# Second attention of a two-layer block: the weighting of the values issued for two key tiles at a time

## The reference, cut to what matters

```python
q = input_tensor @ wq.T + bq          # the same for k and v
q = q.reshape(B, S, H, D).transpose(0, 2, 1, 3)
scores = jnp.einsum('bhsd,bhtd->bhst', q, k) / jnp.sqrt(jnp.float32(D))
attn = jax.nn.softmax(scores, axis=-1)
out = jnp.einsum('bhst,bhtd->bhsd', attn, v)
out = out.transpose(0, 2, 1, 3).reshape(B, S, E)
return out @ wo.T + bo
```

## Time and profile before

| what | value |
|---|---|
| median of 3 runs | 2039.92 us (2038.96 to 2041.53) |
| profiled execution, its own time | 2040.23 us |
| profiled execution, span from first to last instruction | 2038.5 us |
| busy share of the span: PE, PEld, DVE, ACT, POOL | 93%, 72%, 71%, 63%, 32% |
| first weighting of the second attention starts at | 1441.24 us |
| last call of `weigh` inside a group starts at | 2016.66 us |

### The profile page before, as it was taken

The page is one execution under the profiler, slowest core; times in us unless marked ns, Lnnn a source line. Parts: engine busy times, 40 slices in busy tenths (PEclk is TensorE's granted clock), DMA queues, the critical chain, the costliest instruction groups (busy, mean ns, idle before and its releaser), DMA issues. The chain is left out here.

```text
span 2038.5 us, 33530 instructions
## 1 busy us (share of the span) xinstructions
PE 1894.3 (93%) x12080; PEld 1465.6 (72%) x12080; DVE 1445.4 (71%) x2916; ACT 1282.9 (63%) x3061; POOL 648.3 (32%) x1021
## 2 busy tenths in 40 slices
PE   1999999999999999999999789997999999999997
PEld 1888878878888888787788568885555655655653
DVE  5785885886868868858768554445777777777773
ACT  3675674665756756746657465543777677777784
POOL 0353453543543534535435413221001111111112
PEclk9999999999999999999999999996999999999999
DMA  6110211111102111111111293321001011011001
GB/s 228 42 42 22 53 42 32 42 32 43 42 22 52 42 27 47 43 32 42 32 36 41 71 335 132 109 86 52 22 1 52 1 52 52 1 52 52 1 32 42
DMA packets 75204, 111.29 MB, mean 55 GB/s; under 512 B 8224, under 2 KB 49568, under 8 KB 74528
## 3 DMA queue, kind: packets, MB, share of 16 engines
q1 hardware_dynamic: 75040, 109.14, 18.3%
HBM read 54.59 MB, written 20.97 MB: 37 GB/s over the span
## 5 line engine op out<-in xcount | busy, mean ns | idle before, releaser
L1565 DVE TENSOR_REDUCE nm<-ps 128x1 f32<-128x512 f32 x512 | 337.0, 687 | 118.5 <-PE ps L1433 114.2
L1659 ACT ACTIVATE pt<-pst 128x512 f32<-128x512 f32 x512 | 296.8, 602 | 144.5 <-PE pst L1441 143.0
L805 POOL TENSOR_SCALAR pr<-pr,rinv 128x128 f32<-128x128 f32 (+3 forms) x512 | 263.1, 533 | 373.7 <-DVE rinv L693 373.7
L573 ACT ACTIVATE pr<-sc,nmax 128x128 f32<-128x128 f32 (+3 forms) x512 | 268.1, 527 | 142.3 <-DVE nmax L682 140.9
L682 DVE TENSOR_REDUCE nmax<-sc 128x1 f32<-128x128 f32 (+3 forms) x512 | 223.0, 484 | 75.4 <-PE sc L409 75.3
L1433 PE MATMUL ps<-kb,qb 96*128 96x512 f32 x512 | 239.8, 471 | 13.5 <-DVE nm L1565 11.2
L811 POOL TENSOR_TENSOR qk<-ra,rb 128x256 f32<-128x256 f32 x256 | 183.0, 735 | 206.8 <-DVE rb L704 171.7
L1441 PE MATMUL pst<-qb,kb 128*128 128x512 f32 x512 | 208.2, 408 | 6.8 <-ACT pt L1659 3.4
L1433 PEld LDWEIGHTS ps<-kb,qb 96*128 96x128 f32 x512 | 98.7, 193 | 145.3 <-issue 84.0
L421 PE MATMUL w<-ident,pr 128*128 128x128 f32 x1280 | 170.6, 280 | 25.6 <-DVE rb L704 19.7
L383 PE MATMUL w<-wq_hi,xt_hi 128*128 128x384 f32 x512 | 183.6, 359 | 2.8 <-DVE xt_lo L676 1.5
(11 more groups left out here) (212 smaller groups left out, 4552.9 us busy)
## 6 DMA issues: line engine op xcount, KB each, us to landing
k<-k SPq DMA_DIRECT2D x256, 128.0 KB, 2.2
raw<-in_w SPq DMA_DIRECT2D x16, 640.0 KB, 5.9
raw<-in_w SPq DMA_DIRECT2D x8, 704.0 KB, 4.2
xa<-in_x SPq DMA_DIRECT2D x2, 2048.0 KB, 13.7
x<-in_x SPq DMA_DIRECT2D x8, 512.0 KB, 3.9
x_scratch<-x SPq DMA_DIRECT2D x8, 512.0 KB, 2.9
xt_hi_scratch<-xt_hi SPq DMA_DIRECT2D x1, 4096.0 KB, 14.6
xt_lo_scratch<-xt_lo SPq DMA_DIRECT2D x1, 4096.0 KB, 23.8
```

The lines of the kernel that those rows point to most:

```text
L573: act.activation(pr[:, h, SOFF[i]:SOFF[i] + (i + 1) * P], sc[:, bank, at:at + (i + 1) * P], ACT.Exp, bias=nmax[:, h, i:i + 1], accum_out=r ...
L805: pool.tensor_scalar(p, p, rinv[:, h, i:i + 1], 1.0, ALU.mult, ALU.mult).then_inc(scaled, 1)
L1565: dve.tensor_reduce(nm[:, g % 2, i, h:h + 1], ps[:, i % 2, :], AXX, ALU.max, negate=True).then_inc(max_done, 1)
L1659: act.activation(pt[:, g % 2, h, i, :], pst[:, i % 2, :], ACT.Exp).then_inc(exp_done, 1)
```

## The change

`weigh` is called only behind heads 1 and 3 of a group, each time for the two key tiles h-1 and h in a row, where before it was called behind each head for the key tile h. The calls, their operands and waits, and the order of the key tiles stay; no other instruction moves against another, and the four calls behind the last group stay as they are.

```diff
@@ -1528,8 +1528,9 @@
                                     if i < 2 and not last:
                                         pe.wait_ge(stack_done, 6 * (q + 2) + 5 + i)
                                     out_project(b - 1, i)
-                        if back1:
-                            weigh(q - 1, (g + 3) % NG1, h, b + 1 if g else b)
+                        if back1 and h % 2:
+                            for kt in (h - 1, h):
+                                weigh(q - 1, (g + 3) % NG1, kt, b + 1 if g else b)
 
                 for j in range(4):
                     turn_z(0, j, (qn_done, 2 * NT) if j < 2 else (stack_done, j - 1))
```

## The result

The changed kernel took 2043.95 us (median of 20 runs, 2038.14 to 2047.51) against 2040.03 us for the kernel before in the same sessions (20 runs). The ratio is 1.0018, 95% interval 1.0011 to 1.0025: slower by 3.9 us, interval 2.2 to 5.1. The forecast was 2046, slower by 5.9; that lies inside the stated range of 2037 to 2053 and above the measured interval.

What follows compares the result with a forecast made beforehand. No engine alone was taken as the bound: three pass two banks each to and fro, and long weighting bursts starve the other two. Half-group changes sum to +0.76 us a batch, times 7.75 is 5.9 on 2040.0: 2046 us, range 2037 to 2053.

Steps and rivals of the forecast that it cites:

- The double burst, 1.86, and 0.34 us saved a merge: TensorE: two weightings in a row take 1.86 us to the next start, saving 0.14 plus 0.20 of edges.
- rival 1: TensorE alone sets the pace, 0.34 us saved at each of 62 merges: 2019 us; chance 0.13 in whole or part.
- Second half of a plain group 7.80, since the casts lose their cover: Heads 2 and 3, groups 3 and 0: ScalarE's casts delay head 3's exponentials and `pst`, 7.80 against 7.15, +0.65 us.
- The walk: Second half of a plain group followed from the double burst's start through ScalarE's casts and exponentials: next burst at 7.80 us.
- First half of a plain group 8.71 by ScalarE's chain: Heads 0 and 1: the 0.52 wait for VectorE goes, ScalarE's copies and exponentials set 8.71 against 9.23, -0.52 us.
- Group 1's second half 14.46: Half with three projections: casts and head 3's exponential make the third `pst` wait until 12.70; 14.46 against 13.79, +0.67 us.
- Its first half 11.2: Group 1, heads 0 and 1: -0.52 plus some 0.4 for ScalarE's later `vs` copy, -0.1 from 11.31 us.
- Group 3's first half no change: Heads 0 and 1 of group 3: the same ScalarE chain gives 8.71 against 8.69 us, 0.0.
- Group 2's second half +0.05: Half with four output projections: TensorE has enough own work to stand over the casts; +0.05 on 9.90 us.
- Times 7.75 batches: The +0.76 us a batch was multiplied by 7.75 batches (31 groups) to 5.9 us; last group and tail unchanged.
- Rival 2: Gain and loss cancel: the same walk with second halves at +0.45 instead of +0.65, 2041 us; chance 0.18.
- Rival 3: Longer burst covered nowhere: second halves +0.86, first halves no gain, +27, 2067 us; chance 0.09 in whole or part.

Runs made afterwards that it cites:

- light kernels: Kernel before and changed kernel, each with VectorE's maxima and ScalarE's exponentials over only 256 of 512 columns: 2018.8 us with single weightings, 2009.75 us merged.
- run 3: Changed kernel with ScalarE's four casts of head 3 moved from ahead of that head's first exponential to behind its second: 2035.38 us against 2040.62 for the kernel before.
- run 4: Kernel before, single weightings kept, with ScalarE's four casts moved behind the second exponential of head 3: 2047.64 against 2040.62 us, ratio 1.0037.
- light kernel with the casts out of the way: Changed kernel with maxima and exponentials over 256 of 512 columns and ScalarE's casts behind head 3's second exponential: 2001.06 us, ratio 0.981 to the kernel before.
- light single kernel: Kernel before, weighting behind each head, with maxima and exponentials over only 256 of 512 columns: 2018.8 us, ratio 0.989.
- run 1: Kernel before with only heads 0 and 1 merged, tiles 2 and 3 still alone behind heads 2 and 3: 2040.4 against 2040.62 us, ratio 1.0004.
- light merged kernel: Changed kernel with maxima and exponentials over only 256 of 512 columns: 2009.75 us, ratio 0.9851 to the kernel before.

## Why the prediction was right, step by step

- *The double burst, 1.86, and 0.34 us saved a merge.* The 1.86 is right. The 0.34 was too much: the light kernels show 0.21 between heads 2 and 3, 0.32 between heads 0 and 1, and with a wait that goes 0.27 as the mean of a batch. It isn't a term of the forecast's sum; it stands in rival 1 and in the bounds.
- *Second half of a plain group 7.80, since the casts lose their cover.* Right: 7.78, with the wait at the `pst` matmuls of head 3 as said, one `pst` earlier than the step I wrote down as decisive. The walk had the fourth `pst` wait until 7.35 and the burst come 0.45 behind it; in the trace the third waits until 6.86, the fourth starts at 7.44 without a wait of its own, and the burst comes 0.34 behind it. That the total fits to 0.02 is partly luck, since the two errors cancel. Runs 3 and 4 show that the casts are the cause of most of it; the length of the burst has a part too, by way of VectorE (run 3).
- *First half of a plain group 8.71 by ScalarE's chain.* Right: 8.72. The stall for VectorE is gone as said.
- *Group 1's second half 14.46.* Right: 14.44, with the third `pst` of head 3 as the waiting one, at 12.67 for 12.70. *Its first half 11.2*: 11.21, though the 0.4 for the `vs` copy was my estimate, and no run tests it by itself. *Group 3's first half no change*: 8.72 for 8.69.
- *Group 2's second half +0.05.* Mis-sized: 9.83, -0.07. There I had only chosen between bounds. With it the batch is +0.62 in place of +0.76.
- *Times 7.75 batches.* This was the larger error for the traces. The six whole batches give 3.7 us, and the last one with the tail 0.6; in it the last three groups, with less other work, got shorter by 0.8, and the four last calls come 0.86 later behind the last pair. The first one came out shorter, 73.2 against 75.1 us. That isn't an effect to rely on: the start of the second attention runs partly at the lower granted clock, and in the kernel before this reached into its group 1 (1436.77 to 1462.14, clock 0.94), which in the changed kernel ran at full clock:

```profile
1436.77:1462.14 25.37, 24.76 (x133) 16.80 (x132) 16.17 (x28) 13.44 (x26) 1.44 (x2) 0.94 0.12 42
```

```profile
1439.52:1463.46 23.94, 23.16 (x134) 15.98 (x132) 16.39 (x29) 12.93 (x26) 1.41 (x2) 1.00 0.14 44
```

  The first row is the kernel before, the second the kernel after, columns as in the earlier trace rows. By parts these 1.4 us are -2.30 in heads 0 and 1 (10.47 to 8.17 us), +0.56 in heads 2 and 3 and +0.31 up to the next group. Of the 2.30, about 1.13 is the burst that the change takes from head 0, which the first batch doesn't pay for at its start, since no burst stands there yet. The rest, some 1.2 us, is my estimate of what the clock gave: in the kernel before, the first 4.47 us of this stretch ran at a mean granted clock of 0.66, in the one after all of it at 1.00. The medians, +3.9 us, would fit 3.7 + 0.6 and little from the first batch; only one execution of each kernel has a trace, so this isn't shown.
- *Rival 1, TensorE alone*: fell for this kernel and comes near only in the light kernel with the casts out of the way (17.7 us under the light single one, for 21). What the Trainium skill says in "TensorEngine Tiling (Array Packing)", section Tiling Modes, of the drain at a change of mode isn't contradicted: the runs show 0.27 us a merge saved, as a mean. No run takes the drain apart from the rest of an edge.
- *Rival 2, gain and loss cancel*: not held. Its plain second halves would be +0.45, and they are +0.63; the interval of the ratio excludes no change. But 3.9 us is just under the 4.1 that I took as the bound, and the measured 2044 lies between this rival's 2041 and my 2046.
- *Rival 3, the longer burst is covered nowhere*: fell. First halves got shorter by 0.51 to 0.63 in groups 0 and 2, and plain second halves grew by 0.63, not 0.86.
- What the forecast did not see is that its halves aren't separate accounts. It charged +0.65 to the second half; run 1 shows that merging in the first half alone also charges 0.86 to the head behind it. The sum of both was right because each half of the changed kernel was walked with both edits in place.

## What to carry to other kernels

When three engines pass double-buffered banks to and fro, a busy share of 96% doesn't make TensorE the bound: walk one period with starts, and ask at each long burst what the others have queued then. Fewer and longer bursts save switches, but a burst belongs where its neighbours have private work (here four casts, or two casts and two maxima); moving it off such work cost more here than the switch saved. A gain that only appears when a neighbour is made lighter tells which neighbour to reorder, and the same instructions in a better place gave 15 us.

## What the runs showed of the hardware that I had not expected

- Over the six whole batches every half of a group repeats to 0.02 us in the changed kernel and to 0.05 in the one before, while the execution times of the same kernel scatter by several us. In the two profiles, the stretch ahead of the second attention differed by 3.4 us for the same program.
- The exponentials over 256 columns take 0.40 us against 0.60 over 512 (the first is a row of the light merged kernel, the second of the earlier trace rows), so halving the columns takes only a third off:

```profile
1561.86 0.40 ACT L1661 ACTIVATE pt<-pst 128x256 f32<-128x256 f32 x1
```
